# A transformer forward pass on one core: band matrices built in the router's waits, joint cos/sin products, and a streamed normalisation in the second layer

## The chip, the cores and the metric

The kernel runs on one core of a Trainium2 chip. The metric is the device time of one execution in microseconds, as the median of the runs. The engines are called by their names in the profile: PE is TensorE (matrix products and transposes), DVE is VectorE, ACT is ScalarE, POOL is GpSimd, SP is SyncE, which here only starts transfers. Each engine works through its own queue in order and waits on semaphores of the others.

## What is computed

X has 8 patch tiles of 128 rows and 512 columns. Each of four layers adds to X an attention-like part and a feed-forward part of the normalised X. Two parts matter here. Layer 0's feed-forward is a router with low-rank experts. Layer 1's first part is a channel attention whose mask comes from the context:

```
crucial_features = mask * x ; subcrucial_features = (1 - mask) * x        # x: normalised X
c_max, c_avg = max and mean over channels of crucial_features              # s_max, s_avg alike
A = sigmoid(relu(batchnorm(conv1d(concat(max, avg), w, taps=7))))          # once for c, once for s
X = X + crucial_features * A1 + subcrucial_features * A2
X = X + (x @ W_base.T + b + sum over the top 2 of 8 experts of lora)       # x: normalised X, layer 1's feed-forward
```

The mean and the variance of the batch normalisation go over all positions of all tiles. Layer 3 has an attention with rotary position factors cos and sin, gathered by position ids, and keys and values made from the context.

## The kernel before

The whole program is one straight line of instructions for each engine, written out in `program()`. The order of each queue is fixed by hand; semaphores join the queues. fp32 products are made as three products of high and low parts (`mm3`, lines 413 to 418), the high part being a rounded copy made by ACT and the low part the difference, made by POOL or DVE. The weights come as 128 x 512 units: SP loads a unit into one of 5 stage buffers (`unit_step`), ACT makes its high part (`hi_step`, L1213), POOL its low part (`lo_step`, L1036) in one of 10 ring slots. `load.upto(n)`, `hi.upto(n)` and `lo.upto(n)` stand in the queues where the units up to n are due.

**Filler work.** Layer 3's keys and values depend on the context only. They are cut in 32 pieces of 12 matmuls (`kv_pe`), which stand between other work on PE; ACT evicts each (`kv_act`, L814) and SP stores it (`store_kv`). A piece may only start when the one two before it is evicted. `bank_kv` says which PSUM banks it uses.

**Layer 0's router** (`router_dve(v, 0, ...)`, `router_act`, `router_low_pe`, `router_turn_pe`): PE makes the logits and the experts' low products, DVE subtracts the row's maximum (L628 to L632), ACT takes exp (L600) and copies the second half of the low products (L602), DVE normalises (L647 to L651), PE turns the scores (L755), DVE multiplies (L658) and ACT and DVE split the product in high and low parts. Beside it ACT and POOL split the context in its high parts (L1345) and low parts (`cTl`, L1084), which the first four pieces need.

**Layer 1's channel attention.** DVE normalises all eight tiles (L464 to `xnf`). For each tile PE transposes it (L2129), DVE splits it by the mask `crucial` (L1694, L1695) and takes two maxima (L1697, L1698), and ACT takes the sums with accumulating copies (L1376) to `rows`. Then DVE builds the six 128 x 128 band matrices of the convolution from a shifted diagonal (`band`, L612 to L621), 26 instructions after the shift, each waiting for the one before. PE convolves (L2144), and DVE, PE, POOL and ACT in turn make mean, variance, root, relu and sigmoid (L1707 to L1729). DVE forms each tile's channel factors, `gT = crucial * (A1 - A2) + A2` (L1737), PE transposes them (L2156), and DVE multiplies them by `xnf` (L1746) and adds to X (L1747). The statistics of the next normalisation go along. After all eight tiles the normalisation itself runs: `ln_row` on DVE (L464), `ln_turn` on PE (L497), `ln_act` (L517), `ln_low` (L479), with the router's logits between.

**The cos/sin products** (`tables_pe`, L2117): four rounds; in each POOL makes a one-hot of 256 position ids (`one_hot`, L1093, one buffer), PE multiplies both 512 x 128 tables by it and ACT copies the results to `cosT` and `sinT` (`tables`, L1362). The first round stands behind layer 0's router, the others behind the splits, each followed by a piece; the convolution comes behind the last of them and behind `su_rc` 4.

## Time and profile before

| | |
|---|---|
| median of 3 runs | 1456.38 us (1453.41 to 1458.69) |
| the profiled execution's own time | 1461.52 us |
| its span, first to last instruction | 1459.7 us |
| PE busy | 1322.6 us (91%) |
| DVE busy | 959.1 us (66%) |
| ACT busy | 594.0 us (41%) |
| POOL busy | 548.5 us (38%) |
| mean granted PE clock | 0.966 of full |
| the chain that ended last, by engine | PE 63%, DVE 17%, issue 7%, POOL 6%, ACT 4% |

A matmul's records overlap, so a busy PE is not a PE at its peak. The granted clock is either 1.00 (2.4 GHz) or 0.50 (1.2 GHz); a mean between them is a mix. The page by 40 slices of 36.5 us shows the stretch of this change as slices 8 to 11, where PE is at 8 to 9 tenths. Times in the text are from the span's start.

### The profile page before, as it was taken

What the parts mean: (1) busy time and instruction counts of PE and PEld (TensorE: products, weight loads), DVE (VectorE), ACT (ScalarE), POOL (GpSimd) and SP (SyncE); (2) the same over time, 40 slices, a digit from 0 to 9 for tenths busy, and PEclk for the clock granted to TensorE, in tenths of its full rate; (3) what the DMA queues carried; (4) which work ended last, traced back from release to release, by engine and by line L of the source; (5) the groups of instructions that cost most, each with busy time, mean ns of one, the idle gap of its engine ahead of it and who ended that gap; (6) DMA issues with size and microseconds to landing.
All of it is one profiled execution on the core that took longest, in us unless ns stands there. A gap on an engine that the chain in (4) does not pass through costs nothing.

```text
span 1459.7 us, 20660 instructions
## 1 busy us (share of the span) xinstructions
PE 1322.6 (91%) x6958; PEld 996.1 (68%) x6958; DVE 959.1 (66%) x2109; ACT 594.0 (41%) x1614; POOL 548.5 (38%) x548
## 2 busy tenths in 40 slices
PE   2888877988899999999999899999999999999797
PEld 1555544767677777677878777777777777777565
DVE  6999956596633688843222566777777777677745
ACT  2777773361312344433121324344343444344341
POOL 5001003642313444142221444464554645445274
PEclk9999887998999999999999999999999999999999
DMA  5211111211221000031110131011111111110001
GB/s 168 59 30 43 31 25 63 87 66 65 73 80 51 1 8 30 1 95 51 38 56 23 51 100 52 30 58 51 37 58 59 58 41 46 51 37 30 1 1 58
DMA packets 53610, 71.68 MB, mean 49 GB/s; under 512 B 5936, under 2 KB 24689, under 8 KB 53507
## 3 DMA queue, kind: packets, MB, share of 16 engines
q1 hardware_dynamic: 52592, 69.15, 15.0%
q10 hardware_dynamic: 914, 1.22, 0.3%
q8 instruction: 57, 0.93, 0.3%
q14 instruction: 47, 0.38, 0.1%
HBM read 55.67 MB, written 10.49 MB: 45 GB/s over the span
## 4 chain that ended last, share of the span: by engine, by line
PE 63%; DVE 17%; issue 7%; POOL 6%; ACT 4%; DMA 2%; SPq 1%; POOLq 0%; DVEq 0%; ACTq 0%
PE bank L413 15%; PE bank L418 14%; PE bank L417 14%; PE bank L2399 3%; DVE topv L1603 2%; PE bank L2279 2%; PE bank L2375 2%; POOL ring_l L1036 2%; PE bank L2261 2%; DVE top L1597 2%; PE bank L2386 1%; DVE bank L1883 1%; DVE xn L1863 1%; DVE xn L1849 1%; POOL probs L1183 1%
## 5 line engine op out<-in xcount | busy, mean ns | idle before, releaser
L1036 POOL TENSOR_TENSOR ring_l<-stage,ring_h 128x512 fp32r<-128x512 f32 x137 | 181.9, 1346 | 250.5 <-ACT ring_h L1213 250.5
L413 PE MATMUL bank<-xTh_b,ring_h 128*128 128x512 f32 x464 | 189.9, 409 | 4.4 <-issue 3.0
L417 PE MATMUL bank<-xTl_b,ring_h 128*128 128x512 f32 x464 | 184.3, 397 | 0.0
L418 PE MATMUL bank<-xTh_b,ring_l 128*128 128x512 f32 x464 | 184.3, 397 | 0.0
L1158 POOL TENSOR_TENSOR q<-xn 128x512 f32<-128x512 f32 x64 | 82.6, 1291 | 205.6 <-DVE xn L1863 205.6
L413 PE MATMUL bank<-ring_h,o3h 128*128 128x512 f32 x256 | 125.3, 490 | 3.5 <-issue 3.5
L1507 ACT ACTIVATE probsT<-bank 128x512 f32<-128x512 f32 x64 | 38.2, 598 | 203.4 <-PE bank L2386 203.4
L1519 ACT ACTIVATE probs<-bank,nbias 128x128 f32<-128x128 f32 x256 | 90.5, 366 | 51.0 <-DVE nbias L1885 51.0
L413 PEld LDWEIGHTS bank<-xTh_b,ring_h 128*128 128x128 f32 x464 | 88.0, 190 | 25.0 <-issue 6.4
L418 PEld LDWEIGHTS bank<-xTh_b,ring_l 128*128 128x128 f32 x464 | 87.7, 189 | 21.5
L418 PE MATMUL bank<-ring_h,o3l 128*128 128x512 f32 x256 | 101.6, 397 | 0.0
L417 PE MATMUL bank<-ring_l,o3h 128*128 128x512 f32 x256 | 100.6, 393 | 0.0
L417 PEld LDWEIGHTS bank<-xTl_b,ring_h 128*128 128x128 f32 x464 | 88.0, 190 | 18.3
L1863 DVE TENSOR_TENSOR xn<-bank,sinT 64x512 f32<-64x512 f32 x128 | 88.1, 688 | 1.7
L1213 ACT ACTIVATE ring_h<-stage 128x512 fp32r<-128x512 f32 x137 | 81.8, 630 | 17.2 <-DMA stage<-in_units_dram 16.9
L1895 DVE TENSOR_TENSOR o3l<-bank,o3h 128x512 fp32r<-128x512 f32 x64 | 44.3, 692 | 58.3 <-ACT o3h L1529 58.3
L1877 DVE TENSOR_TENSOR X<-X,bank 128x512 f32<-128x512 f32 x64 | 44.0, 687 | 52.2 <-PE bank L418 51.8
L1814 DVE TENSOR_TENSOR hid<-silu,bank 128x512 f32<-128x512 f32 x22 | 15.1, 688 | 93.9 <-PE bank L418 86.3
L2375 PEld LDWEIGHTS bank<-k,q 128*128 128x128 f32 x512 | 67.7, 193 | 7.0 <-issue 1.7
L1183 POOL TENSOR_TENSOR probs<-probs,rsums 128x512 f32<-128x512 f32 x64 | 66.6, 1040 | 15.4 <-DVE rsums L1891 15.4
L2399 PE MATMUL bank<-probsT,v 128*128 128x512 f32 x128 | 67.2, 606 | 4.8 <-ACT probsT L1507 4.8
L2375 PE MATMUL bank<-k,q 128*128 128x128 f32 x512 | 68.3, 277 | 0.3 <-POOL q L1158 0.3
(332 smaller groups left out, 3249.4 us busy)
## 6 DMA issues: line engine op xcount, KB each, us to landing
stage<-in_units_dram SPq DMA_DIRECT2D x137, 256.0 KB, 3.0
ring_l<-k SPq DMA_DIRECT2D x64, 64.0 KB, 2.1
raw_k<-kvs SPq DMA_DIRECT2D x16, 256.0 KB, 2.1
kraw<-raw_k SPq DMA_DIRECT2D x16, 256.0 KB, 3.5
v<-raw_v SPq DMA_DIRECT2D x16, 256.0 KB, 2.8
stage<-in_context_dram SPq DMA_DIRECT2D x8, 256.0 KB, 2.9
raw_v<-kvs SPq DMA_DIRECT2D x8, 256.0 KB, 2.0
out_dram<-X SPq DMA_DIRECT2D x8, 256.0 KB, 2.0
```

The source lines that it names most:

```text
L413: ins = nc.tensor.matmul(out_ap, wh, mh, start=start, stop=False)
L417: nc.tensor.matmul(out_ap, wh, ml, start=False, stop=False)
L418: return nc.tensor.matmul(out_ap, wl, mh, start=False, stop=stop)
L1036: nc.gpsimd.tensor_tensor(ring_l[:, place_of(u), :], stage[:, u % STAGE, :], f32(ring_h[:, place_of(u), :]), ALU.subtract).then_inc(w_lo, 1)
L1158: nc.gpsimd.tensor_tensor(dst, xn[:, (at - 1) % 2, :], xn[:, 2 + (at - 1) % 2, :], ALU.add).then_inc(a3_ad, 1)
L1183: nc.gpsimd.tensor_tensor(pb, pb, rsums[:, n % 4, :].unsqueeze(2).to_broadcast((P, 4, P)), ALU.mult).then_inc(a3_pn, 1)
L1213: nc.scalar.activation(ring_h[:, place_of(u), :], stage[:, u % STAGE, :], ACT.Copy).then_inc(w_hi, 1)
L1519: ins = nc.scalar.activation(probs[:, n % 3, c], bank[n % 2][:, c], ACT.Exp, bias=nbias[:, n % 4, r:r + 1], scale=-1.0, accum_out=psums[:, ...
L1863: ins = nc.vector.tensor_tensor(xn[to, 2 + i % 2, :], src[fro, :], sinT[to, c], ALU.mult)
L1895: nc.vector.tensor_tensor(o3l[:, m % 2, :], bank[3 + m % 2][:], f32(o3h[:, m % 2, :]), ALU.subtract).then_inc(a3_ol, 1)
L2375: ins = nc.tensor.matmul(bank[n % 2][:, r * P:(r + 1) * P], q3[:, r, c], k3[:, c], start=True, stop=True)
L2399: nc.tensor.matmul(bank[3 + m % 2][:], v3[:, m % 8, :], probsT[:, m % 3, :], start=True, stop=True).then_inc(a3_pv, 1)
```

## The change

It touches layer 0's router and layer 1's channel attention, up to layer 1's router.

- The bands are no longer built behind the splits. The first three are built on DVE ahead of the wait for layer 0's logits, the other three after its scores, ahead of the wait for the turned scores.
- The cos and sin tables have 64 different columns each (sin's sign aside), so one 512 x 128 table holds both. A round is 4 products in place of 8. ACT writes the four halves of `cosT` and `sinT` for 512 positions at a time, with the sign. The rounds move: the second stands behind the transposes of tiles 0 and 1, the third behind those of tile 5, the fourth behind piece 9. They use banks 5 and 4, and the pieces 4 to 11 banks 6 and 7.
- The convolution comes directly behind the fourth round. Pieces 10 and 11 go behind the statistics.
- The channel factors are made by ACT with a scale and a bias for each partition, not by DVE. Their buffers are other tiles. The product with `xnf` is made in place.
- The normalisation of a tile follows its update, one tile later on DVE, and two tiles later on PE and three on DVE for the low part. The pieces 12 to 18 stand between; POOL takes the root of each tile by itself.
- SP loads one unit further ahead from piece 8 to piece 17.

```diff
         def router_dve(v, i, n_next):
+            if i == 0:
+                for k in range(3):
+                    band(v, k)
             v.wait_ge(f_t, 3 * i + 1)
...
                 nc.vector.tensor_tensor(low[:, cut, :]... .then_inc(f_ls, 1)
+            if i == 0:
+                for k in range(3, 6):
+                    band(v, k)
             for j in range(2):
...
-            first = 0 if i < 4 else 6 if i < 18 else 4 if i < 24 else 0
+            first = 0 if i < 4 else 6 if i < 12 else 4 if i < 24 else 0
...
-                load.upto(unit_kv(i) + (10 if i >= 18 else 5))
+                load.upto(unit_kv(i) + (10 if i >= 18 else 6 if i >= 8 else 5))
...
             lo.upto(8)
             one_hot(1)
+            one_hot(2)
             lo.upto(9)
-            one_hot(2)
             one_hot(3)
...
-            lo.upto(U_L1F)
-            ln_pool(g, LN_L1F[0])
+            lo.upto(12)
+            for b in range(B):
+                ln_root(g, LN_L1F[0], b)
+                if b < 2:
+                    lo.upto(13 + b)
...
+            def tables(half):
+                a.wait_ge(su_rope, 2 * half + 2)
+                c = slice(half * HALF, (half + 1) * HALF)
+                low_rows, high_rows = slice(0, 64), slice(64, P)
+                for to in (low_rows, high_rows):
+                    nc.scalar.activation(cosT[to, c], bank[5 - half][low_rows, :], ACT.Copy)
+                nc.scalar.activation(sinT[low_rows, c], bank[5 - half][high_rows, :], ACT.Copy, scale=-1.0)
+                nc.scalar.activation(sinT[high_rows, c], bank[5 - half][high_rows, :], ACT.Copy).then_inc(su_rc, 1)
...
-                if b in (3, 5, 7):
-                    kv_act(a, 6 + (b - 1) // 2)
-                if b in (4, 6):
-                    hi.upto(7 + b // 2)
+                if b in (2, 4, 6):
+                    kv_act(a, 6 + b // 2)
+                if b in (3, 5):
+                    hi.upto(9 + b // 5)
+            kv_act(a, 10)
+            tables(0)
             tables(1)
-            kv_act(a, 10)
-            tables(2)
...
-            hi.upto(11)
+            hi.upto(12)
             a.wait_ge(x_rows, 3)
             nc.scalar.activation(zz[:, :, :], z[:, :, :], ACT.Exp, scale=-1.0).then_inc(x_e, 1)
...
+            def gains_by_channel(b):
+                if b >= 2:
+                    a.wait_ge(x_gp, b - 1)
+                else:
+                    a.wait_ge(x_rows, 4)
+                for q in range(4):
+                    i = 4 * b + q
+                    ins = nc.scalar.activation(gT[b % 2][:, q * P:(q + 1) * P], crucial[:, i, :], ACT.Identity,
+                                               scale=gains[:, 2, i:i + 1], bias=gains[:, 1, i:i + 1])
+                ins.then_inc(x_gt, 1)
+            gains_by_channel(0)
+            kv_act(a, 12)
+            for b in range(B):
+                if b + 1 < B:
+                    gains_by_channel(b + 1)
+                if b < 2:
+                    hi.upto(13 + b)
+                else:
+                    kv_act(a, 11 + b)
+                    ln_act(a, LN_L1F[1], xTh_a, b - 1, b - 2)
...
-            for i in range(6):
-                band(v, i)
             v.wait_ge(x_sum, B)
...
+            for b in range(B + 3):
+                if b < B:
+                    v.wait_ge(x_gp, b + 1)
+                    link(v, v_chain, nc.vector.tensor_tensor(xnf[:, b, :], bank[b % 2][:], xnf[:, b, :], ALU.mult))
+                    nc.vector.tensor_tensor(X[:, b, :], X[:, b, :], xnf[:, b, :], ALU.add).then_inc(x_done, 1)
+                    ln_one(v, LN_L1F[0], b)
+                if 1 <= b <= B:
+                    ln_row(v, *LN_L1F, b - 1)
+                if b >= 3:
+                    ln_low(v, LN_L1F[1], b - 3, xTh_a, xTl_a)
...
@@ TensorE
-                for i in range(2):
-                    for k in range(KT):
-                        ins = nc.tensor.matmul(bank[5 - 3 * (q % 2)][:, i * 256:(i + 1) * 256], tabs[:, i, k, :], hot[:, k, :],
+                for k in range(KT):
+                    ins = nc.tensor.matmul(bank[5 - q // 2][:, q % 2 * 256:(q % 2 + 1) * 256], tabs[:, k, :], hot[:, k, :],
...
+                if b == 1:
+                    tables_pe(1)
+                if b in (2, 4, 6):
+                    kv_pe(t, 6 + b // 2)
+                if b == 5:
+                    tables_pe(2)
             kv_pe(t, 10)
-            tables_pe(2)
-            kv_pe(t, 11)
             tables_pe(3)
-            kv_pe(t, 12)
-            t.wait_ge(su_rc, 4)
             t.wait_ge(x_rows, 1)
...
-            kv_pe(t, 13)
+            kv_pe(t, 12)
             for b in range(B):
                 t.wait_ge(x_gt, b + 1)
                 if b >= 2:
                     t.wait_ge(x_done, XD_L1X + b - 1)
...
-                if 1 <= b <= 5:
-                    kv_pe(t, 13 + b)
+                if b >= 2:
+                    kv_pe(t, 11 + b)
+                    if b == 2:
+                        t.wait_ge(c_ev, 12)
+                    ln_turn(t, LN_L1F[1], b - 2)
+            kv_pe(t, 19)
+            ln_turn(t, LN_L1F[1], 6)
+            t.wait_ge(x_done, XD_L1X + 7)
+            router_logits_pe(t, 1, 0, xTh_a, xTl_a)
+            kv_pe(t, 20)
+            ln_turn(t, LN_L1F[1], 7)
+            kv_pe(t, 21)
+            router_logits_pe(t, 1, 1, xTh_a, xTl_a)
```

## Rows read from the trace of the kernel before

**Rows 1.** Stages with the work between; windows: stretch, length, busy us (instructions) by engine, clock.

```profile
288.00:338.00 50.00, 42.85 (x203) 35.19 (x201) 38.01 (x80) 28.18 (x148) 21.03 (x29) 0.93 0.18 61
338.00:354.00 16.00, 12.02 (x39) 9.17 (x40) 12.94 (x38) 1.50 (x4) 3.50 (x4) 0.68 0.07 27
354.00:388.00 34.00, 29.27 (x154) 22.56 (x153) 27.86 (x60) 11.54 (x21) 11.98 (x20) 1.00 0.34 116
```

**Rows 2.** TensorE, timeline: start, us, engine line op, tiles, idle before, releaser.

```profile
384.76 1.03 PE L497 MATMUL bank<-ident,xn 128*128 128x128 f32 x8
387.46 0.39 PE L413 MATMUL bank<-xTh_a,wrh 128*8 128x512 f32 x1 [1.67 <-DVE xTl_a L479]
```

**Rows 3.** TensorE, timeline, the convolution.

```profile
334.99 2.76 PE L2144 MATMUL bank<-rows,bands 128*128 128x32 f32 x24
```

**Rows 4.** Windows of line 2117 alone, one round: TensorE busy, its weight loads, clock.

```profile
284.98:288.60 3.62, 3.61 (x16) 2.85 (x15) 1.00 0.02 5
```

**Rows 5.** ScalarE, timeline, behind the router's difference.

```profile
266.46 0.26 ACT L600 ACTIVATE sc<-lg 128x64 f32<-128x64 f32 x1 [4.88 <-DVE lg L632]
...
268.25 0.60 ACT L814 ACTIVATE kvs<-bank 128x512 f32<-128x512 f32 x1 [1.05 <-PE bank L418]
271.05 0.60 ACT L814 ACTIVATE kvs<-bank 128x512 f32<-128x512 f32 x1 [2.20 <-PE bank L418]
```

**Rows 6.** VectorE, timeline, from the router to the channel factors.

```profile
261.11 0.23 DVE L628 TENSOR_TENSOR lg<-bank,br 128x64 f32<-128x64 f32 x1 [6.58 <-PE bank L727]
...
261.63 4.80 DVE L632 TENSOR_TENSOR lg<-lg,rt 128x64 f32<-128x64 f32 x1
...
277.09 1.29 DVE L658 SCALAR_TENSOR_TENSOR lows<-bank,lows 128x512 f32<-128x512 f32 x2 [8.56 <-PE bank L755]
...
300.85 0.68 DVE L1694 TENSOR_TENSOR cf<-bank,crucial 128x512 f32<-128x512 f32 x1
...
316.68 0.48 DVE L612 TENSOR_SCALAR probs<-iota,con 128x512 f32<-128x512 f32 x1
...
337.79 0.23 DVE L1707 COPY z<-bank 128x64 f32<-128x64 f32 x1 [9.53 <-PE bank L2144]
...
342.22 1.23 DVE L1721 TENSOR_SCALAR zs<-zs,conv 128x2 f32<-128x2 f32 x1 [1.13 <-POOL zs L1108]
...
345.59 3.19 DVE L1737 TENSOR_SCALAR gT<-crucial,gains 128x128 f32<-128x128 bf16 x8
```

**Rows 7.** VectorE, groups by line and form, 316 to 328: busy us, mean ns.

```profile
L621 DVE SCALAR_TENSOR_TENSOR bands<-probs,conv,bands 128x128 f32<-128x128 f32 x20 | 7.8, 390 | 0.7
```

**Rows 8.** GpSimd, timeline.

```profile
255.54 2.43 POOL L1084 TENSOR_TENSOR cTl<-probs,cTh 128x1024 fp32r<-128x1024 f32 x1
...
296.77 3.63 POOL L1093 TENSOR_SCALAR hot<-probs,con 128x256 f32<-128x256 int32 x4
```

**Rows 9.** All engines, timeline, in layer 3.

```profile
912.57 0.99 DVE L1847 SCALAR_TENSOR_TENSOR xn<-kraw,cosT 128x512 f32<-128x512 f32 x1
912.97 1.73 POOL L1036 TENSOR_TENSOR ring_l<-stage,ring_h 128x512 fp32r<-128x512 f32 x1
...
913.57 1.67 DVE L1849 SCALAR_TENSOR_TENSOR xn<-kraw,sinT 64x512 f32<-64x512 f32 x1
```

**Rows 10.** Windows of all instructions, columns as in rows 1.

```profile
298.10:304.80 6.70, 5.03 (x14) 4.19 (x15) 6.53 (x11) 6.27 (x42) 2.30 (x3) 0.50 0.00 0
```

**Rows 11.** TensorE, timeline, the transpose of tile 3.

```profile
299.77 1.09 PE L2129 MATMUL bank<-ident,xnf 128*128 128x128 f32 x4 [2.01 <-DVE cf L1695]
```

**Rows 12.** ScalarE, groups by line and form, 288 to 340.

```profile
L1376 ACT ACTIVATE junk<-cf 128x128 f32<-128x128 f32 x64 | 18.8, 296 | 2.3 <-DVE cf L1695 2.3
```

**Rows 13.** ScalarE, timeline, in layer 0.

```profile
152.49 0.88 ACT L1301 ACTIVATE probs<-bank,nbias 128x128 f32<-128x128 f32 x3
```

**Rows 14.** VectorE, timeline, one tile of layer 0.

```profile
239.35 0.68 DVE L1675 TENSOR_TENSOR X<-X,bank 128x512 f32<-128x512 f32 x1
...
241.94 0.68 DVE L1675 TENSOR_TENSOR X<-X,bank 128x512 f32<-128x512 f32 x1
```

More of the change, by code:

```diff
@@ L79, in constants @@
     inv = (1.0 / np.float32(10000.0) ** (np.arange(0, P, 2, dtype=np.float32) / np.float32(P))).astype(np.float32)
-    ang = np.concatenate([t * inv, t * inv], 1).astype(np.float32)
-    sin = np.sin(ang)
-    sin[:, :64] *= -1
-    tabs = np.stack([np.cos(ang), sin]).astype(np.float32).reshape(2, KT, P, P)
+    ang = (t * inv).astype(np.float32)
+    tabs = np.concatenate([np.cos(ang), np.sin(ang)], 1).astype(np.float32).reshape(KT, P, P)
     rep = np.zeros((P, 8, P), np.float32)
@@ L700, in kv_pe @@
                     t.wait_ge(c_ev, i - 1)
+                if i == 12:
+                    t.wait_ge(su_rc, 2)
                 o = bank_kv(i)[:]
@@ L1718, in _ @@
             v.wait_ge(x_tot, 2)
-            nc.vector.tensor_copy(zs[:, 3, :], bank[4][:, 0:2]).then_inc(x_rows, 1)
+            nc.vector.tensor_copy(zs[:, 3, :], bank[3][:, 2:4]).then_inc(x_rows, 1)
             v.wait_ge(x_rs, 1)
@@ L1728, in _ @@
             link(v, v_chain, nc.vector.reciprocal(gains[:, 0:2, :], zz[:, :, :]))
-            link(v, v_chain, nc.vector.tensor_tensor(gains[:, 2, :], gains[:, 0, :], gains[:, 1, :], ALU.subtract))
-            def gains_by_channel(b):
-                if b >= 2:
-                    v.wait_ge(x_gp, b - 1)
-                for q in range(4):
-                    i = 4 * b + q
-                    ins = nc.vector.tensor_scalar(gT[:, b % 2, q * P:(q + 1) * P], crucial[:, i, :], gains[:, 2, i:i + 1],
-                                                  gains[:, 1, i:i + 1], ALU.mult, ALU.add)
-                ins.then_inc(x_gt, 1)
-            gains_by_channel(0)
-            for b in range(B):
-                if b + 1 < B:
-                    gains_by_channel(b + 1)
-                v.wait_ge(x_gp, b + 1)
-                link(v, v_chain, nc.vector.tensor_tensor(tmpx[:, b % 2, :], bank[b % 2][:], xnf[:, b, :], ALU.mult))
-                nc.vector.tensor_tensor(X[:, b, :], X[:, b, :], tmpx[:, b % 2, :], ALU.add).then_inc(x_done, 1)
-                ln_step(v, LN_L1F[0], b)
-            ln_step(v, LN_L1F[0], B)
-            ln_step(v, LN_L1F[0], B + 1)
-            ln_dve(v, *LN_L1F, xTh_a, xTl_a)
+            nc.vector.tensor_tensor(gains[:, 2, :], gains[:, 0, :], gains[:, 1, :], ALU.subtract).then_inc(x_rows, 1)
+            for b in range(B + 3):
[8 more added lines that the diff above has]
+                    ln_low(v, LN_L1F[1], b - 3, xTh_a, xTl_a)
             router_dve(v, 1, LN_L2X[0])
@@ L2112, in tables_pe @@
                 t.wait_ge(s_rest, 96)
-                if q >= 2:
-                    t.wait_ge(su_rc, q - 1)
-                for i in range(2):
-                    for k in range(KT):
-                        ins = nc.tensor.matmul(bank[5 - 3 * (q % 2)][:, i * 256:(i + 1) * 256], tabs[:, i, k, :], hot[:, k, :],
-                                               start=k == 0, stop=k == KT - 1)
+                for k in range(KT):
+                    ins = nc.tensor.matmul(bank[5 - q // 2][:, q % 2 * 256:(q % 2 + 1) * 256], tabs[:, k, :], hot[:, k, :],
+                                           start=k == 0, stop=k == KT - 1)
                 ins.then_inc(su_rope, 1)
@@ L2147, in _ @@
                 t.wait_ge(x_zs, j + 1)
-                nc.tensor.matmul(bank[3 + j][:, 0:2], ones_f[:, :], zs[:, 1 + j, :], start=True, stop=True).then_inc(x_tot, 1)
-            kv_pe(t, 13)
+                nc.tensor.matmul(bank[3][:, 2 * j:2 * j + 2], ones_f[:, :], zs[:, 1 + j, :], start=True, stop=True).then_inc(x_tot, 1)
+            kv_pe(t, 12)
             for b in range(B):
@@ L2155, in _ @@
                     c = slice(k * P, (k + 1) * P)
-                    ins = nc.tensor.transpose(bank[b % 2][:, c], gT[:, b % 2, c], ident[:, :])
+                    ins = nc.tensor.transpose(bank[b % 2][:, c], gT[b % 2][:, c], ident[:, :])
                 ins.then_inc(x_gp, 1)
-                if 1 <= b <= 5:
-                    kv_pe(t, 13 + b)
-            t.wait_ge(c_ev, 18)
-            router_pe(t, 1, LN_L1F[1], U_L1F, xTh_a, xTl_a)
+                if b >= 2:
[11 more added lines that the diff above has]
+            router_logits_pe(t, 1, 1, xTh_a, xTl_a)
+            t.wait_ge(c_ev, 21)
+            router_low_pe(t, 1, 0, U_L1F, xTh_a, xTl_a)
+            router_turn_logits_pe(t, 1)
+            router_low_pe(t, 1, 1, U_L1F, xTh_a, xTl_a)
             def base1(b):
```

53 lines of the change are left out of this document (14 added, 39 removed).

## The prediction

> **What bounds the kernel now.** I read the table by stages first, then the timelines of TensorE, VectorE and GpSimd. Only the stretch from 254 to 388 us is touched: layer 0's router, layer 1's channel attention and the start of layer 1's feed-forward. From 288 us on TensorE is busy 43 of 50 us, then 12 of 16 at a mean clock of 0.68, then 29 of 34 [rows 1]: no engine is full, and a chain handed from engine to engine sets the end. Its last common point is the second half of layer 1's router logits, at 387.46 [rows 2]. By then both orders have issued the same 21 key/value pieces and the first half of the logits. What this point gains, the end gains, because the work behind it keeps its order. The chain is: X of layer 0, its normalisation, eight crucial/rest splits on VectorE, 27 band instructions there, convolution at 334.99 [rows 3], statistics, channel factors, eight updates, a whole normalisation, logits. Beside the bands stand three rounds of cos/sin products (3.6 us each, [rows 4]) and pieces of 2.8 us (two evictions are 2.80 us apart, [rows 5]).
>
> **Part 1, bands in the router's waits.** From behind the splits go the shift, at 316.68 [rows 6], and 26 band instructions, 20 of them at 0.39 us [rows 7]: with their links 11.1 us, and VectorE's next work stands in line behind them. They go to two holes of VectorE, 6.58 us (up to 261.11) and 8.56 us (up to 277.09) [rows 6]. By the 0.39 us of one [rows 7] and their number, 14 and 13, the first three bands take 5.9 us and the last three 5.2. Both fit by length. But in the first hole GpSimd subtracts from SBUF to SBUF without a gap: one instruction of 1.3 us, then from 255.54 four of 2.43, then one of 1.3, until 266.4 [rows 8]. L632 reads two SBUF tiles of 64 elements, took 4.80 us there and ended with GpSimd's block [rows 6]. In layer 3 a pair shows the same as turns: L1847 ended at 913.56, GpSimd's 1.3 us subtraction beside it was stretched to 1.73, and L1849, of as many columns as L1847, took 1.67 [rows 9]. So the two take turns at best. Each band instruction then waits for one of GpSimd's: six of the 14 get through by 267.5, the other eight need 3.0 us, to 270.5, and the router's difference follows at 271.3 in place of 266.43. If none gets in until 266.4, that becomes 273.0. If all slip in between, it stays at 266.4.
>
> Who waits: in ScalarE's queue exp (L600), the second half of low and the first key/value eviction stand behind the difference; together they need 1.3 us (0.26 and twice 0.6, [rows 5]). TensorE may run two pieces meanwhile and no more, since the third needs the first one's bank. Now the four pieces run from 265.1, the end of the fourth 2.43, to 276.4. With turns the low halves of the context are done at 266.0, pieces one and two end at 271.6, and the third starts at 271.3 + 1.3 = 272.6: all four end at 278.2, **1.7 us late**. With none getting in the third starts at 274.3 and the end is 3.5 late, and TensorE has idled 3.5 us. A fall of the clock then costs about half of each spell: after two gaps of 2.0 us there came 6.7 us at 0.50 [rows 10, 11]. I take **2.3 us** (turns, and a spell that falls mostly into TensorE's new wait), bounds 0 and 6.9. The last three bands end 7.4 us after the difference (exp 0.3, sums and products 1.9, bands 5.2), at 278.7, when the turned scores arrive too: no cost.
>
> A rule of the Trainium skill speaks against this part ("SBUF — State Buffer", section "Who interferes with whom"): a VectorE instruction with two SBUF inputs, or in a two-port mode, contends for an exclusive lock with a GpSimd instruction that reads SBUF. By that rule the trace's L632 and L1849 agree. Without it part 1 would be put at 0.
>
> **Part 2, joint cos/sin products.** Of the 16 matmul records of a round (3.61 us, [rows 4]) eight go, 1.8 us, in four rounds: 7.4 us less on TensorE. ScalarE copies the two 512-column halves in four 64-row pieces each; at 0.60 us for 512 columns [rows 5] that is 4.8 us, in a stretch where it waits anyway. One of two table loads on SyncE goes. But the second round is moved: on TensorE it now stands behind the transposes of patch tiles 0 and 1 and ahead of those of tile 2. It needs the second one-hot from GpSimd, which is in line behind eight roots and a subtraction and ends at 300.40 now (296.77 + 3.63) [rows 8]; I take 300.1. TensorE idles from 293.5 and its clock falls, as it does now [rows 10]. The round then takes 2 x 1.8 = 3.6 us, the four transposes 0.9 (eight take 1.03 at the full clock, [rows 2]), so tile 2 is there at 304.6. VectorE takes it at 300.85 now [rows 6]: a **new stall of 3.8 us**. The next piece must also be done before tile 3 (308.2), another 0.9. From there VectorE's 2.64 us a tile lead ((316.68 - 300.85) / 6), and the last split ends at 321.5. ScalarE's eight sums of it (0.296 us each, [rows 12]) end at 323.1; today the bands hide them. The scaling adds 0.45.
>
> **Part 3, convolution behind the rows.** It starts at 323.6 for 334.99 and ends at 326.4 (2.76 us, [rows 3]), 11.35 us ahead. Pieces 10 and 11 go behind the statistics. These take 7.8 us now (337.79 to 345.59), of which L1721 was blocked about 1.05 by a subtraction [rows 6]. Two subtractions are ready there after the change, so I add 1.25 us, bounds 0 and 1.3: factors may start at 326.4 + 7.8 + 1.25 = 335.45. TensorE idles through most of 3.2 us and does pieces 10 and 11 (5.6 us) largely at the lower clock, from 329.6 to 337.6; bounds 335.2 and 340.8.
>
> **Part 4, channel factors by ScalarE.** VectorE loses 32 instructions (eight took 3.19 us, [rows 6]). On ScalarE three with one operand by partition took 0.88 us [rows 13], four so 1.13; with two I take 1.45, bounds 1.13 and 2.0. The queue behind is what counts: factors 0, evictions of pieces 10 and 11 (338.2), factors 1 (339.7), one high part, factors 2 (341.75), transposes of tile 2 done at 342.4. TensorE's work is thin from 337.6, so I give the next piece a spell at the lower clock: it ends at 346.3, not 345.2.
>
> **Part 5, streamed normalisation.** From tile 3 (346.8) each turn of TensorE is four transposes 0.6, a piece 2.8, four transposes 0.45: 3.85 us. VectorE's is the product, 0.7, and what it does for a tile of layer 0 in 2.6 us (239.35 to 241.94: sum, statistics, row, low part, [rows 14]): 3.3. ScalarE's is 1.45 + 0.6 + 0.6. TensorE leads: five turns to 366.05, piece 18 and transposes to 369.3, logits 372.1, piece 19, the last transposes 375.4, piece 20 at 378.2; the last low part is there at 376.8. SyncE's loads run one unit further ahead from piece 8 on: each waits for a subtraction long done but unit 19's, about 371.5, wanted after 385. Hidden; uncovered it is 1 to 3 us.
>
> **The sum.** 387.46 - 378.2 = 9.3 us without part 1, less 0.4 for a dearer ScalarE: 8.9. Less 2.3: **6.6 us**. From the profiled execution's 1461.5 (its span is 1459.7) that gives 1454.9. It lies 5.1 above the median of the three runs, 1456.4, so I predict **1449.8**.
>
> **Rivals.** (a) GpSimd keeps VectorE out until 266.4, TensorE idles 3.5 us and then runs at half clock: part 1 costs 5.2 to 6.9, the gain is 2 to 3.7, time 1453.5. For it: L632 lost two hand-overs. Against: L1847 won its own. (b) The bands slip through, and the clock holds at tile 2: gain 10 to 12, time 1445.5. Against: GpSimd's block has no gap. (c) The ramp behind the early convolution gives it back: a factor group takes 2.0 us, pieces 10 and 11 end at 340.8, and 4.9 of the gain goes: 1454. (d) Slower: short transposes and waits keep TensorE at 1.2 GHz through the streamed loop. Its 31 us of work there lose 1.7 us for each 3.4 us at the lower level; 13 us of it beyond what I counted use up the 6.6 us, and 24 us give 1461.7. Against: from 354 to 388 the same kinds of work ran at 1.00 with 15% idle [rows 1].
>
> **How the numbers follow.** The forecast (1446.5 to 1452.5) has 0.50, (a) 0.16, (b) 0.12, (c) 0.13, (d) 0.09. The range, 1443.5 to 1457.5, takes in (a), (b), (c) and half of (d). A measurement tells 0.3%, 4.4 us, from no change: below 1452.0 lie (b) and nearly all of the forecast, 0.60; within lie its rest, (a), (c) and some of (d), 0.29; slower 0.11.
>
> **What would show it.** Right: the difference ends between 270.5 and 273, in turns with GpSimd; an idle TensorE before the second cos/sin round and a VectorE wait of some 4 us before the third split; the convolution ends 8 to 10 us before 337.75; TensorE hardly waits from tile 3 on. Wrong: the difference still ends at 266; or the clock is 0.50 for over 13 us in the loop; or VectorE ends most of TensorE's waits there.

## The result, and the profile after

The changed kernel takes 1452.34 us (median of 20 executions), the kernel before in the same comparison 1458.36 (also 20). The ratio is 0.9957 (95% interval 0.9945 to 0.9970), which is 6.3 us less; the medians differ by 6.0. The prediction said 6.6 us less and 1449.8 us. It had taken the 1456.38 us of three executions for the kernel before, 2.0 less than the median of the twenty. The profiled execution's span is 1453.4 us for 1459.7.

The single terms of the sum did not all come out as their total did. The stages first (columns as in [rows 1]; the mean granted clock of TensorE is the third figure from the right):

```profile
288.00:338.00 50.00, 40.34 (x181) 33.45 (x180) 36.06 (x73) 29.97 (x149) 25.29 (x36) 0.83 0.16 54
338.00:354.00 16.00, 12.85 (x56) 9.90 (x55) 11.34 (x20) 11.13 (x27) 6.02 (x10) 0.79 0.18 66
354.00:388.00 34.00, 34.00 (x175) 25.71 (x174) 17.15 (x36) 16.26 (x35) 7.35 (x12) 1.00 0.32 109
```

From 354 us on TensorE is now busy without a gap, where it was idle 4.7 us before [rows 1]: the last stage is bound by TensorE. The first stage got worse: its mean granted clock fell from 0.93 to 0.83. VectorE's timeline of the first hole, for [rows 6]:

```profile
254.33 1.41 DVE L610 TENSOR_SCALAR probs<-iota,con 128x512 f32<-128x512 f32 x1
255.78 2.33 DVE L617 TENSOR_SCALAR bands<-probs,conv 128x128 f32<-128x128 f32 x1
258.14 4.84 DVE L619 SCALAR_TENSOR_TENSOR bands<-probs,conv,bands 128x128 f32<-128x128 f32 x2
263.01 2.33 DVE L617 TENSOR_SCALAR bands<-probs,conv 128x128 f32<-128x128 f32 x1
265.38 3.21 DVE L619 SCALAR_TENSOR_TENSOR bands<-probs,conv,bands 128x128 f32<-128x128 f32 x6
...
270.23 0.23 DVE L633 TENSOR_TENSOR lg<-lg,rt 128x64 f32<-128x64 f32 x1
```

An instruction of 0.3 to 0.4 us takes 2.33 to 2.42 here, one for each of the four large subtractions that GpSimd makes (they start at 255.42, 257.97, 260.35 and 262.78). Behind GpSimd's last one the rest run at 0.37. The difference ends at 270.46 in place of 266.43. TensorE's timeline, then VectorE's, for the wait at the second round, the convolution, and the end of the stretch [rows 2, 3]:

```profile
301.41 3.73 PE L2114 MATMUL bank<-hot,probsT 128*128 128x256 f32 x8 [5.46 <-POOL hot L1087]
...
324.48 4.47 PE L2140 MATMUL bank<-rows,bands 128*128 128x32 f32 x24 [2.03 <-DVE rows L1715]
...
342.23 0.88 PE L2152 MATMUL bank<-ident,probsT 128*128 128x128 f32 x4 [1.98 <-ACT probsT L1396]
344.29 1.11 PE L2152 MATMUL bank<-ident,probs 128*128 128x128 f32 x4 [1.17 <-ACT probs L1396]
...
380.57 0.40 PE L411 MATMUL bank<-xTh_a,wrh 128*8 128x512 f32 x1
```

```profile
305.62 0.69 DVE L1708 TENSOR_TENSOR cf<-bank,crucial 128x512 f32<-128x512 f32 x1 [2.50 <-PE bank L2126]
...
308.86 0.69 DVE L1708 TENSOR_TENSOR cf<-bank,crucial 128x512 f32<-128x512 f32 x1 [0.51 <-PE bank L2126]
...
324.15 0.27 DVE L1715 TENSOR_SCALAR rows<-rows 128x32 f32<-128x32 f32 x2 [2.01 <-ACT junk L1374]
```

TensorE waits 5.46 us for the one-hot and then makes the round at half clock (3.73 us; the first round took 1.89). The convolution too runs at half clock for the most part, with a mean of 0.61 over its 4.47 us. VectorE stalls 2.50 and 0.51 us for it. The second half of layer 1's router logits starts at 380.57, 6.9 us ahead of 387.46 [rows 2].

The normalisation in front of the splits has a smaller delay, which the prediction did not have. VectorE's last two instructions of it, in the kernel before and then in the changed one, and GpSimd's subtraction in the changed one:

```profile
294.49 1.17 DVE L464 TENSOR_SCALAR xnf<-X,mv,rstd 128x512 f32<-128x512 f32 x2 [0.44 <-POOL rstd L445]
```

```profile
295.86 1.99 DVE L462 TENSOR_SCALAR xnf<-X,mv,rstd 128x512 f32<-128x512 f32 x2 [0.44 <-POOL rstd L443]
296.31 1.26 POOL L1030 TENSOR_TENSOR ring_l<-stage,ring_h 128x512 fp32r<-128x512 f32 x1
```

In the kernel before GpSimd was idle until 295.41, when VectorE was nearly through. In the changed kernel the subtraction starts in the middle of the two, and they take 0.8 us longer. bands_back and shift_psum show the same 1.99 us. That GpSimd holds them is read from the overlap; no run moved the subtraction.

### The profile page after: what moved, and what is told of

It reads as the page before. It is cut to its first block, busy times and chain, and to the rows that moved or that the text cites. A ratio compares the mean times of both kernels' runs of the same rounds, so it can differ in the third digit from the quotient of the medians.

```text
span 1453.4 us, 20595 instructions
## 1 busy us (share of the span) xinstructions
PE 1317.1 (91%) x6926; PEld 994.1 (68%) x6926; DVE 957.2 (66%) x2077; ACT 608.1 (42%) x1646; POOL 550.1 (38%) x548
## 4 chain that ended last, share of the span: by engine, by line
PE 63%; DVE 17%; issue 6%; POOL 6%; ACT 5%; DMA 2%; SPq 1%; POOLq 0%; DVEq 0%; ACTq 0%
PE bank L411 15%; PE bank L415 14%; PE bank L416 14%; PE bank L2407 3%; DVE topv L1617 2%; PE bank L2287 2%; PE bank L2383 2%; POOL ring_l L1030 2%; PE bank L2269 2%; DVE top L1611 2%; PE bank L2394 1%; DVE bank L1883 1%; PE bank L495 1%; DVE xn L1863 1%; DVE xn L1849 1%
## 5 line engine op out<-in xcount | busy, mean ns | idle before, releaser
L1883 DVE COPY_PREDICATED bank<-mask,big 128x512 f32<-128x512 int32 x64 | 59.7, 933 | 13.5 <-PE bank L2383 13.5
```

Of the source, the lines that this page charges most:

```text
L1883: link(v, v_chain, nc.vector.copy_predicated(s4, mask3[:, b, :].unsqueeze(1).to_broadcast((P, 4, P)), big[:, :].unsqueeze(1).to_broadcast( ...
```

## Experiments

All ratios are to the kernel before. The executions differ by some us in stretches that no edit touches, so each profile is also read by the length of one **stretch**: from the first transposes of layer 0's normalisation (before 233.10, after 232.83 us) to layer 1's turned scores (418.42 and 411.55). It was 185.3 us before and 178.7 in the changed kernel. A stretch comes from one execution and is not free of chance. Up to the first cos/sin round round_late is the changed kernel, instruction for instruction, yet its round starts 53.1 us into the stretch and not 54.8, as the router's spell at half clock did not come. A difference of less than 1 us between two stretches is weak evidence.

| kernel | ratio (95% interval) | stretch, us |
|---|---|---|
| the changed kernel | 0.9957 (0.9945 to 0.9970) | 178.7 |
| bands_back | 0.9996 (0.9984 to 1.0008) | 186.2 |
| bands_alone | 1.0023 (1.0004 to 1.0042) | 187.9 |
| shift_psum | 0.9942 (0.9919 to 0.9965) | 177.9 |
| bands_second | 0.9968 (0.9947 to 0.9988) | 179.1 |
| round_late | 0.9895 (0.9878 to 0.9912) | 174.0 |
| piece_first | 0.9932 (0.9908 to 0.9956) | 177.6 |
| factors_dve | 0.9960 (0.9946 to 0.9975) | 179.5 |
| no_stream | 0.9990 (0.9974 to 1.0005) | 182.3 |
| both_mended | 0.9910 (0.9885 to 0.9935) | 173.0 |
| shared_factors | 0.9890 (0.9872 to 0.9908) | 171.7 |
| diff_psum | 0.9884 (0.9864 to 0.9905) | 172.9 |
| all_four | 0.9871 (0.9850 to 0.9893) | 171.7 |

### What moving the bands is worth

The changed kernel without part 1, and the kernel before with part 1 alone.

```diff
# bands_back
-                for k in range(3):        # ahead of the logits
-                    band(v, k)
...
-                for k in range(3, 6):     # ahead of the turned scores
-                    band(v, k)
...
+            for i in range(6):
+                band(v, i)
             v.wait_ge(x_sum, B)
```

> The changed kernel with all six bands back behind the eight splits, ahead of the wait for ScalarE's sums; everything else stays. Theory (the sum of the prediction, with the changed kernel's own rows): the router's difference ends some 4 us earlier, near 266.5, and the spell at half clock near 281 us does not come, worth 2.6 us; but 11.1 us of bands stand in VectorE's line again where the changed kernel only waits 2.0 us for ScalarE's sums, so the convolution starts 9.1 - 2.6 = 6.5 us later than in the changed kernel, near 331. Nothing behind it gives time back, so the whole is 6 to 7 us longer than the changed kernel, ratio to the kernel before 0.999 to 1.002: the move of the bands is then worth as much as the whole change, and the other four parts together nothing. Rival 1 (the later parts have slack of their own, the streamed loop hides it): ratio 0.996 to 0.998. Rival 2 (a better cover of TensorE by the longer wait, so that the clock holds behind the convolution): ratio 0.998, with the spell at 325 to 335 us gone.

> The kernel before with part 1 alone: three bands ahead of layer 0's logits, three ahead of the turned scores, none behind the splits. Theory (the parts work only together: before, TensorE's queue of rounds and pieces reaches the convolution at 334.99 us, 7.2 us after the last band ends and 6.7 us after the scaling): nothing is gained there, and the turns with GpSimd in the first hole put the router 1.1 to 4 us late; the convolution starts at 335 to 338 us and the whole is 0 to 3 us longer than before: ratio 1.000 to 1.002. Rival (the bands are a cost by themselves wherever they stand behind the splits, 11 us on the chain): 4 us or more shorter, ratio 0.997 or less.

Both theories held. TensorE's timeline at the convolution, bands_back and then bands_alone:

```profile
333.79 5.33 PE L2136 MATMUL bank<-rows,bands 128*128 128x32 f32 x24 [10.12 <-DVE rows L1711]
```

```profile
328.74 3.72 PE L2121 MATMUL bank<-hot,probsT 128*128 128x256 f32 x16 [0.97 <-POOL hot L1099]
...
335.10 2.76 PE L2148 MATMUL bank<-rows,bands 128*128 128x32 f32 x24
```

Without the move TensorE stands 10.12 us in front of the convolution and the gain is gone (0.9996). The convolution starts 3.2 us earlier in the stretch than in the kernel before (98.7 us in for 101.9), but it takes 5.33 us for 2.76, all of it at half clock, and its end is only 0.7 earlier. With the move alone the convolution has no wait in front of it at all: the round and a piece lead up to it, and only the router's delay is left (1.0023). In the kernel before two chains reach the convolution within 7.2 us of each other, VectorE's bands and TensorE's rounds and pieces. Taking away one of them is worth nothing or less; taking away both is worth the whole. The halved cos/sin products (part 2) were not undone by themselves, so their own share is not shown.

### Who keeps VectorE out in the first hole

```diff
# shift_psum, against the changed kernel
-            shift = probs[:, 2, :]
+            shift = bank[3][:, :]
```

> The changed kernel with one name changed: the shifted diagonal, from which the bands are built, lies in a PSUM bank and not in an SBUF tile, so no band instruction has two SBUF inputs. The bands stay where they are. Theory (VectorE and GpSimd take turns at SBUF in the first hole): the first three bands run at 0.4 to 0.5 us an instruction, without the 4.8 and 2.3 us gaps, are done by 262, the logits are taken at 261 to 262 and the difference ends near 266.4 (it has two SBUF inputs itself and still waits for GpSimd's block); the spell near 281 us does not come and the whole is 2 to 2.6 us shorter than the changed kernel: ratio to the kernel before 0.993 to 0.9945. Rival 1 (14 more instructions in the hole cost their length wherever their inputs lie): difference near 270, ratio 0.9955 to 0.996. Rival 2 (PSUM reads of 128 columns are dearer than SBUF's and eat it up, 26 instructions at 0.1 us more): 0.995 to 0.996.

VectorE's timeline of shift_psum:

```profile
255.30 0.35 DVE L617 TENSOR_SCALAR bands<-bank,conv 128x128 f32<-128x128 f32 x1
255.69 0.74 DVE L619 SCALAR_TENSOR_TENSOR bands<-bank,conv,bands 128x128 f32<-128x128 f32 x2
...
261.68 4.81 DVE L633 TENSOR_TENSOR lg<-lg,rt 128x64 f32<-128x64 f32 x1
```

The same instructions, at the same place beside the same GpSimd work, take 0.35 and 0.37 us instead of 2.33 and 2.42. Only where they read from was changed. The difference, with both inputs still in SBUF, takes 4.81 us and ends at 266.49. That is the Trainium skill's rule ("SBUF — State Buffer", section "Who interferes with whom"): an instruction with two SBUF inputs contends with a GpSimd instruction that reads SBUF, and so does one in a two-port mode, which `tensor_scalar` can enter. The trace agrees for both kinds: L619 (2.42 for 0.37) and L617 (2.33 for 0.35). The spell at half clock that the changed kernel has behind its router is gone too (windows 278 to 285 us; the changed kernel, then shift_psum):

```profile
278.00:285.00 7.00, 5.11 (x18) 3.97 (x17) 5.49 (x9) 3.06 (x6) 4.27 (x5) 0.76 0.34 112
```

```profile
278.00:285.00 7.00, 5.56 (x24) 4.50 (x25) 6.38 (x13) 2.73 (x5) 5.24 (x6) 1.00 0.36 112
```

Of the six profiles in which the turns delay the router five have this spell and round_late does not; of the other eight none has it. So the delay makes the spell likely and does not settle it.

The mechanism held; the size did not. The first cos/sin round starts 2.8 us earlier against the stretch's start (285.09 - 233.14 for 287.58 - 232.83), but nothing on the chain waits for that round. VectorE's first split, which is on the chain, starts 1.5 us earlier (63.4 us into the stretch for 64.9), and the convolution 0.9. In between stands the second round, here with the transposes of tile 2 behind it:

```profile
300.20 3.78 PE L2114 MATMUL bank<-hot,probsT 128*128 128x256 f32 x8 [6.76 <-POOL hot L1087]
303.77 1.06 PE L2126 MATMUL bank<-ident,xnf 128*128 128x128 f32 x4
```

Its wait for the one-hot grew from 5.46 to 6.76 us, since the one-hot comes only 1.5 us earlier where TensorE comes 2.8. Behind the longer wait the half clock lasts through the transposes as well, which take 1.06 us for 0.60. The measured ratio's interval (0.9919 to 0.9965) holds this small gain and also the expected 2 us.

```diff
# diff_psum, against both_mended (below); lgp is bank[2][:, 64:128] for layer 0
-            nc.vector.tensor_tensor(lg[:, :, 0:8], lg[:, :, 0:8], rt[:, 0, :]..., ALU.subtract)
+            nc.vector.tensor_tensor(lgp[i], lgp[i], rt[:, 0, :]..., ALU.subtract)
```

> The kernel with both mends and the router's logits of layer 0 kept in PSUM between their bias and ScalarE's exp, so that the difference has one SBUF input (the row's maximum) and not two. Theory (VectorE waits for GpSimd's subtractions only where an instruction has two SBUF inputs): the difference takes 0.22 to 0.3 us and not 4.8, and the next instruction with two SBUF inputs (the scores times the reciprocal sum, 512 columns) waits in its place until GpSimd's last context subtraction or slips in after one of them; all together 0 to 1 us of the total, since the four pieces wait for GpSimd's low halves in any case: ratio 0.989 to 0.991. Rival (the 64-column difference waits for something else, such as the bank or a semaphore): it still ends with GpSimd's block, 4.8 us.

VectorE's timeline of diff_psum:

```profile
259.17 0.23 DVE L635 TENSOR_TENSOR bank<-bank,rt 128x64 f32<-128x64 f32 x1
...
260.19 4.82 DVE L654 TENSOR_TENSOR low<-sc,rt 128x512 f32<-128x512 f32 x2
```

The difference takes 0.23 us. The wait falls on the next instructions with two SBUF inputs, the two products of the scores: they take 4.82 us for 1.29. The rival is out. For the whole it is worth nothing that the stretch shows (172.9 for 173.0): the four pieces wait for GpSimd's low halves in any case.

```diff
# bands_second, against the changed kernel
-                for k in range(3):        # ahead of the logits
-                    band(v, k)
...
-                for k in range(3, 6):
+                for k in range(6):        # ahead of the turned scores
```

> The changed kernel with all six bands in the second hole (ahead of the turned scores), none ahead of the logits. Theory: GpSimd subtracts nothing from SBUF to SBUF there, so 27 instructions run at 0.39 to 0.41 us, 11.1 us in all, against a hole of 8.6 us; the difference ends near 266.5, the products of the scores start about 2.6 us later than in the kernel before and about 2.7 us earlier than the 4.0 us delay of the changed kernel leads to, the wait at 281 us changes place, and the time is within 1 us of the changed kernel: ratio 0.995 to 0.997. Rival (the products of the scores have slack, as TensorE has pieces to run): 1.5 to 2.5 us shorter than the changed kernel, ratio 0.994.

TensorE waits longer in front of layer 0's expert products, 3.40 us where the changed kernel and shift_psum wait 1.89:

```profile
282.13 0.47 PE L411 MATMUL bank<-ring_h,lowT_h 128*128 128x512 f32 x1 [3.40 <-DVE lowT_l L664]
```

The stretch is 179.1 for 178.7, as expected: the turns in the first hole cost about what the overfull second hole costs. No spell at half clock follows the 3.40 us (clock 1.00 from 276 to 286 us).

### The second cos/sin round

```diff
# round_late, against the changed kernel, TensorE's loop over the patch tiles
-                if b == 1:
+                if b == 3:
                     tables_pe(1)
```

> The changed kernel with the second cos/sin round two tiles later on TensorE, behind the transposes of patch tile 3 and not of tile 1. Theory (the round stands in front of tile 2's transposes and waits for the one-hot, so VectorE stalls 2.5 + 0.5 us before the splits of tiles 2 and 3): both stalls go, the last split ends near 319.2 for 322.1, the convolution starts 2.5 to 3 us earlier and the end gains as much: ratio to the kernel before 0.993 to 0.994. Rival 1 (TensorE's idle time before the round and its spell at half clock only move, and the stall comes before tile 4): ratio 0.995 to 0.996. Rival 2 (something behind it, ScalarE's sums or the fourth round, is late instead): convolution less than 1 us earlier.

The splits of tiles 2 and 3 start at 300.43 and 303.07, without a wait and 2.64 us apart, and so on to the last. VectorE's timeline, then TensorE's:

```profile
300.43 0.68 DVE L1708 TENSOR_TENSOR cf<-bank,crucial 128x512 f32<-128x512 f32 x1
...
303.07 0.68 DVE L1708 TENSOR_TENSOR cf<-bank,crucial 128x512 f32<-128x512 f32 x1
```

```profile
318.93 3.73 PE L2140 MATMUL bank<-rows,bands 128*128 128x32 f32 x24 [1.09 <-DVE rows L1715]
```

The convolution starts 88.3 us into the stretch for 91.6. Of these 3.3 us 3.0 are the two stalls; the first split already starts 0.4 earlier (64.5 for 64.9), as this execution had no spell behind the router, and that is not the edit's. The convolution is also 0.7 us shorter, and the stretch 4.7. The ratio fell by 9 us, twice that; see the last section. Rival 1 is out: no stall came before tile 4.

```diff
# both_mended = round_late and shift_psum together
```

> The changed kernel with both changes of the first runs: the shifted diagonal in a PSUM bank, and the second cos/sin round behind the transposes of patch tile 3. Theory: with the bands in PSUM alone the router was 1.3 us earlier and the time went into a longer wait for the second one-hot (6.8 us for 5.5 us); with the round out of the way it reaches the splits. The convolution starts 1.3 us earlier than with the late round alone, or 2.6 to 3.5 us earlier if the spell at half clock in the router's last pieces goes with it: ratio to the kernel before 0.987 to 0.989. Rival (eight roots on GpSimd set the start of the splits whatever the router does): the same as with the late round alone, 0.9895.

Against round_late the first cos/sin round starts 0.9 us earlier (52.2 us into the stretch for 53.1), the first split 0.9 (63.7 for 64.5), and the convolution 0.9 (87.4 for 88.3). So with the round out of the way all that the router gains reaches the convolution, as the theory said. It is 0.9 us and not 1.3 to 3.5 because the profile of round_late had no spell to lose. The ratio can't tell the two kernels apart.

### The convolution's clock

```diff
# piece_first, against the changed kernel
             kv_pe(t, 10)
             tables_pe(3)
+            kv_pe(t, 11)
             t.wait_ge(x_rows, 1)
```

> The changed kernel with piece 10 between the fourth cos/sin round and the convolution, and only piece 11 behind the statistics. Theory (the convolution ran at half clock, 4.47 us for 2.76, because TensorE had idled 2.03 us for ScalarE's sums): the piece fills that wait; the convolution starts 0.8 us later and takes 2.8 to 3.0 us, so it ends 0.7 to 0.9 us earlier; the statistics then lie under one piece less, TensorE idles 1 to 2 us more behind them, and the sum is within 1 us of the changed kernel: ratio to the kernel before 0.995 to 0.9965. Rival 1 (the clock stays up for the whole stretch up to 336 us and 2.5 to 3.5 us come back): ratio 0.9935 to 0.9945. Rival 2 (the fall comes all the same, the piece is pure delay): 1 to 2.8 us longer than the changed kernel, 0.9965 to 0.998.

```profile
321.54 2.76 PE L2141 MATMUL bank<-rows,bands 128*128 128x32 f32 x24
```

`kv_pe(t, n)` issues all pieces below n, so the added line moves piece 10. The convolution starts 0.2 us later in the stretch and ends 1.5 earlier, at the full clock. The stretch is 1.1 us shorter. The theory had the parts right and put the sum too low by a little; the ratio (0.9908 to 0.9956) leaves room for rival 1, the stretch doesn't. Over the 14 kernels the same 24 matmuls took 2.76 us with no wait in front (three kernels), 2.87 behind 0.38 us of wait (both_mended), 3.46 to 3.90 behind 1.03 to 1.10 (four), 3.87 to 4.58 behind 2.03 to 2.11 (five) and 5.33 behind 10.12 (bands_back). A wait costs clock each time; how much differs by up to 0.7 us at the same wait.

### The channel factors and the streamed normalisation

```diff
# factors_dve, against the changed kernel: in VectorE's loop, nothing of it on ScalarE
+                    if b + 1 < B:
+                        gains_by_channel(b + 1)      # four tensor_scalar
                     v.wait_ge(x_gp, b + 1)
```

> The changed kernel with part 4 undone: VectorE makes the channel factors, four instructions a tile one tile ahead, in the streamed loop. Theory: VectorE has 3.3 us of work a tile in that loop and gets 4 x 0.4 = 1.6 us more, 4.9 us, against TensorE's 3.7 us a turn; from tile 2 on VectorE leads, six turns are 1.2 us longer, and layer 1's second half of the logits comes 6 to 8 us later than in the changed kernel: ratio to the kernel before 0.9995 to 1.001. Rival (ScalarE's 1.65 us a group is what holds back the first three tiles; VectorE is quicker there and the loop has idle time in it): 1 to 3 us longer, ratio 0.996 to 0.998.

TensorE's and VectorE's timeline of factors_dve in the loop:

```profile
354.64 0.60 PE L2151 MATMUL bank<-ident,probsT 128*128 128x128 f32 x4
...
358.44 0.66 PE L2151 MATMUL bank<-ident,probs 128*128 128x128 f32 x4
...
362.81 0.66 PE L2151 MATMUL bank<-ident,probsT 128*128 128x128 f32 x4 [0.30 <-DVE probsT L1734]
```

```profile
352.94 1.11 DVE L1734 TENSOR_SCALAR probsT<-crucial,gains 128x128 f32<-128x128 bf16 x4
```

The theory fell. (The factors' buffers are named `probs` and `probsT` there.) Four factors cost VectorE 1.11 us here, not the 1.6 of [rows 6], and it enters the loop ahead of TensorE; its 4.4 us a tile lead only from 358 us on. The stretch is 0.8 us longer, less than either theory said, and the ratios can't be told apart (0.9960 and 0.9957): beside the streamed normalisation part 4 did next to nothing.

```diff
# no_stream, against the changed kernel, VectorE (ScalarE and TensorE likewise)
-                if 1 <= b <= B:
-                    ln_row(v, *LN_L1F, b - 1)
-                if b >= 3:
-                    ln_low(v, LN_L1F[1], b - 3, xTh_a, xTl_a)
+            ln_dve(v, *LN_L1F, xTh_a, xTl_a)
```

> The changed kernel with part 5 undone: the updates of all eight tiles first, then the whole normalisation of layer 1, with the factors still made by ScalarE. Theory: a turn of the loop is 0.45 us shorter on TensorE without the transposes, some 2 us in all; the normalisation behind it then has no pieces left beside it and takes 6 to 8 us more than in the changed kernel, so the second half of the logits is 3 to 5 us later: ratio to the kernel before 0.9975 to 0.9995. Rival (streaming moves work from one place to the other and gains nothing, since TensorE has the same 21 pieces in either order): ratio 0.995 to 0.9965.

```profile
354.00:388.00 34.00, 30.79 (x156) 22.92 (x155) 16.78 (x31) 14.26 (x29) 5.97 (x10) 1.00 0.31 109
```

In the last stage TensorE is idle 3.2 us (4.7 in the kernel before, nothing in the changed one), and the stretch is 3.6 us longer than in the changed kernel: inside the theory's 3 to 5.

```diff
# shared_factors, against both_mended
+            v.wait_ge(x_rows, 4)
+            for q in range(4):
+                ins = nc.vector.tensor_scalar(gT[0][:, q * P:(q + 1) * P], crucial[:, q, :], ...)
+            ins.then_inc(x_g0, 1)
...
-            gains_by_channel(0)
+            gains_by_channel(1)
```

> The kernel with both mends and one more edit: VectorE, which waits there for TensorE's transposes anyway, makes the first four channel factors, and ScalarE begins with the second four at the same time. Theory (TensorE waits 2.0 and 1.4 us for ScalarE's factors of tiles 1 and 2): the first wait goes and most of the second, the streamed loop starts 2 to 3 us earlier, and all behind it with it: ratio 0.9885 to 0.9895 where both mends alone gave 0.991 (or 0.9865 to 0.9875 if those are truly at 0.989). Rival (the second wait grows by what the first loses, as tile 2's transposes wait for VectorE's update of tile 0): less than 1 us.

TensorE's timeline of shared_factors, the factors' transposes of tiles 0, 1 and 2:

```profile
336.51 0.60 PE L2158 MATMUL bank<-ident,probs 128*128 128x128 f32 x4
336.95 0.60 PE L2158 MATMUL bank<-ident,probsT 128*128 128x128 f32 x4
339.41 0.66 PE L2158 MATMUL bank<-ident,probs 128*128 128x128 f32 x4 [1.87 <-ACT probs L1397]
```

Tile 2's transposes start 2.9 us behind tile 0's, for 4.7 in both_mended: one wait of 1.87 us in place of 1.98 and 1.40. The stretch is 1.3 us shorter than there. This understates the edit: the convolution, ahead of it, happened to take 3.90 us for 2.87, and from its end on the stretch is 2.3 us shorter, within the theory's 2 to 3. The second wait did grow, by less than the first lost.

```diff
# all_four = diff_psum (with both_mended in it) and shared_factors together
```

> All four edits that helped or did no harm, in one kernel: the shifted diagonal in PSUM, the late second round, the router's logits in PSUM, and the first channel factors shared between VectorE and ScalarE. Theory (the stretches add up, with the rows of the single runs: 174.0 us from the normalisation of layer 0 to layer 1's turned scores with the late round, 1 us less by the diagonal, 1.3 us less by the shared factors): 171.5 to 172 us for that stretch against 185.3 before and 178.7 in the changed kernel, ratio to the kernel before 0.9865 to 0.989. Rival (a gain of one takes that of another, as TensorE's clock falls where it idles less evenly): 173 to 174 us for the stretch, 0.989 to 0.9905.

The stretch is 171.7 us, within the theory's 171.5 to 172, but shared_factors has the same without the logits in PSUM: no gain of that edit shows. The ratio of 0.9871 beats the kernel before by 1.3% and the changed kernel, at 0.9957, by 0.9% if the two ratios are set against each other. The five kernels with the late round lie at 0.9871 to 0.9910 and their intervals overlap, so which of them is best isn't settled by the ratios.

## Why the prediction was right

The difference is right to 0.3 us (to 0.6 by the medians), but partly because two wrong sizes met. The absolute time is 2.5 us above the forecast, 2.0 of it by the higher median of the kernel before.

- **Part 1** went as told, in turns, and in its sizes up to the splits: the difference ends at 270.46 (predicted 271.3), the fourth piece 1.3 us late against the stretch's start (1.7), the first split 2.5 us late (62.5 us into the stretch before, 64.9 after; 2.3 taken). But the turns are not all of that. bands_back and shift_psum, where the router is on time, have 0.8 and 0.9 us of it too, and 0.8 is what the last two instructions of the normalisation lose beside GpSimd; no term of the sum had that. The other 1.5 are the turns and their spell, and the turns without a spell cost 0.9 (round_late against both_mended). The step that was wrong is the one behind: not all of it is passed on past the second round. shift_psum gave back 0.9 us at the convolution, not 2.3. So the real price of the turns was about 1 us.
- **Part 2**: the stall was foreseen with its place (tile 2, then tile 3), 3.8 and 0.9 us predicted, 2.50 and 0.51 measured. The round itself came as the sum had it: in shift_psum it starts at 300.20 and tile 2 is there at 304.87 (300.1 and 304.6 predicted). The stall was less because the splits in front of it were late, by the 0.8 us of the normalisation and by the router. It is 3.0 us at the convolution, the dearest single step of the change. ScalarE's sums end 2.0 us after the last split (1.6 predicted).
- **Part 3**: without part 1 the sum had the convolution go from 323.6 to 326.4, with it from 325.9 to 328.7. It went from 324.48 to 328.95, 1.4 us sooner and 0.3 later. It took 4.47 us for the 2.76 of [rows 3] that the sum used, 1.7 us that were not in it, and they stand where the delay of parts 1 and 2 was taken 1.4 us too long. That is the mis-sized term: behind the wait in front of it, which the same step foresaw, the convolution ran for the most part at half clock. That the two errors nearly cancel is luck.
- **Statistics and factors**: the first factors started at 337.89 (337.75 with part 1). L1733 and L1735 took 1.23 and 1.42 us beside GpSimd's two subtractions, as told. Four factors took ScalarE 1.65 us (1.45 taken, 2.0 the bound).
- **Part 5**: a turn of TensorE took 3.68 us (3.85), the logits came at 380.57 (378.2 + 0.4 + 2.3 = 380.9). Removed, it cost 3.6 us. TensorE leads from tile 3 on as told.
- **The rivals**: (a) did not come, the bands got in one by one. (b) would have needed gaps; the clock fell. (c) came in small part: a factor group took 1.65 us, between the forecast's 1.45 and the rival's 2.0, but pieces 10 and 11 were done at 339.6, as the forecast has it with part 1 (337.6 + 2.3 = 339.9) and not the rival (340.8 + 2.3 = 343.1). (d) did not come: the mean clock was 0.57 from 342 to 350 us, about 7 of these 8 us at half clock, and 1.00 from 354 to 388. What no rival named is that the change holds a stall of its own which costs half as much as the change gains; the prediction counted it, but did not ask what the order of the round was worth.

## What to carry to other kernels

Where two chains met at one wait with 7 us between them, shortening one gave nothing: look for the other's last releaser before moving work off the first. Work put into an engine's wait must be read for its neighbours as well as for its length: here one operand in PSUM let VectorE run beside a GpSimd that works in SBUF (0.37 us for 2.42). And work that is moved to an engine's idle time must not wait itself for a slow producer ahead of something due: here moving one round two tiles back took 4.7 us off a stretch that the whole change had shortened by 6.6.

## What the runs showed of the hardware

- **Hand-overs.** A band instruction got in behind every one of GpSimd's subtractions (2.33, 2.42 us apiece), but the 64-column difference did not: issued at 261.68 in shift_psum, it was done only at 266.49, past two ends of GpSimd instructions (4.81 us; 4.80 in [rows 6]). Nor did the first 512-column product of the scores in diff_psum, issued at 260.19: GpSimd's subtraction ended at 262.62, but the two products (0.6 us each) were done only at 265.01, behind the next one as well. Both read a second input that is repeated along its last axis, the bands do not; whether that decides it was not tried and stays open.
- **The clock of a short group.** The convolution's 24 small matmuls took 2.76 to 5.33 us by the wait in front of them, as listed above. The length of a wait alone does not foretell a spell: the router's products ran at half clock behind 1.89 us in the changed kernel, but not behind 1.89 in shift_psum and round_late or behind 3.40 in bands_second.
- **Spells elsewhere.** From the turned scores of layer 1 to the end of the span all kernels run the same work, yet it took 1035.4 us (bands_alone) to 1047.9 (bands_second); in the latter one stretch has a mean clock of 0.72 where the changed kernel has 0.94 (windows; bands_second, then the changed kernel):

```profile
440.00:470.00 30.00, 26.72 (x122) 23.30 (x121) 9.80 (x16) 9.78 (x18) 8.92 (x7) 0.72 0.21 61
```

```profile
440.00:470.00 30.00, 26.72 (x146) 22.35 (x145) 11.72 (x18) 10.62 (x20) 8.94 (x7) 0.94 0.21 62
```

  In the profile of round_late this part took 1037.1 us and in the changed kernel 1041.9 (1041.3 before); what lies ahead of the stretch, nearly the same work in all, took 230.6 and 232.8 us (233.1 before). So some of the 15.3 us by which round_late's ratio beats the kernel before may lie there, and the 11.3 us of its stretch are the part that is explained. Whether an edit at 300 us moves the spells behind 420 us in every execution, or only by chance, the runs don't settle.
